# A three-layer decoder on one core: self slots in another order, a passage in another order, and idle TensorE on the identity at two places

## The reference

```
x = x + self_attention(layernorm(x))       # causal, 16 heads of 8, q = k = v = the normalised x
x = x + cross_attention(layernorm(x), ctx) # biased scores: q k^T + bias[b, h], projections Wq, Wk, Wv, Wo
x = x + ffn_block(layernorm(x))            # attention with projections, then a second norm,
                                           # a gate (argmax of 8 experts), expert w1, relu, w2
```

## Time and profile before

| what | us |
|---|---|
| median of 3 runs (lowest, highest) | 417.43 (417.13, 418.52) |
| the profiled execution, and its span | 417.45, 415.6 |
| start, to the first mask on VectorE (0 to 14.7): PE / DVE / ACT / POOL busy | 5.00 / 8.24 / 4.03 / 11.67 |
| self slots (14.7 to 74.8, 60.1 long) | 45.56 / 39.58 / 35.05 / 27.16 |
| passage (74.8 to 100.5, 25.7 long) | 17.84 / 17.35 / 10.34 / 11.57 |
| cross attention (100.5 to 200, 99.5 long) | 88.50 / 85.77 / 54.56 / 93.03 |
| last attention (200 to 310, 110 long) | 93.11 / 59.58 / 56.68 / 64.35 |
| gate and places (310 to 338, 28 long) | 12.74 / 10.24 / 5.94 / 4.23 |
| scatter of the rows (338 to 361.8, 23.8 long) | 0.01 / 1.03 / 0.00 / 15.66 |
| expert tiles (361.8 to 410, 48.2 long) | 47.19 / 34.02 / 24.80 / 21.06 |

### The profile page before, as it was taken

The page is one execution under the profiler, slowest core; times in us unless marked ns, Lnnn a source line. Parts: engine busy times, 40 slices in busy tenths (PEclk is TensorE's granted clock), DMA queues, the critical chain, the costliest instruction groups (busy, mean ns, idle before and its releaser), DMA issues.

```text
span 415.6 us, 9925 instructions
## 1 busy us (share of the span) xinstructions
PE 310.0 (75%) x3435; PEld 202.8 (49%) x3435; DVE 256.1 (62%) x614; ACT 191.4 (46%) x372; POOL 250.3 (60%) x354
## 2 busy tenths in 40 slices
PE   2677769568889999988788788888776400199993
PEld 0233335235666666656344444444444300199993
DVE  6667675667989999995357455656521340067772
ACT  2454566524655556554364365464661200045551
POOL 7943343276999889999958556673421237324453
PEclk9899999988999999999899899999995555589997
DMA  6103345003488787421139950000000012323430
GB/s 169 35 2 103 103 136 175 22 14 101 148 190 225 166 209 180 68 25 17 15 46 272 279 180 3 2 2 2 2 2 2 0 38 101 100 56 96 107 90 19
DMA packets 67041, 36.37 MB, mean 87 GB/s; under 512 B 36253, under 2 KB 56864, under 8 KB 66992
## 3 DMA queue, kind: packets, MB, share of 16 engines
q1 hardware_dynamic: 57040, 15.79, 17.8%
q10 hardware_dynamic: 8448, 16.78, 13.8%
q0 software_dynamic: 1504, 3.16, 2.2%
HBM read 28.48 MB, written 7.69 MB: 87 GB/s over the span
## 4 chain that ended last, share of the span: by engine, by line
PE 37%; POOL 26%; issue 16%; DVE 13%; ACT 5%; DMA 2%; POOLq 0%; DVEq 0%; ACTq 0%
PE pair_banks L605 24%; POOL biased L456 11%; PE work_bank L605 5%; POOL k_lane L433 4%; POOL routed_rows L588 4%; DVE pair_banks L1111 3%; PE small_bank L608 3%; POOL rstd L421 2%; DVE rowmax L1104 2%; PE small_bank L605 2%; PE work_bank L608 1%; ACT probs L944 1%; POOL shift L428 1%; POOL x_sb L482 1%; ACT outT L950 1%
## 5 line engine op out<-in xcount | busy, mean ns | idle before, releaser
L944 ACT ACTIVATE probs<-pair_banks 128x1024 f32<-128x1024 f32 x96 | 97.5, 1022 | 63.2 <-PE pair_banks L605 28.6
L456 POOL TENSOR_TENSOR biased<-biased,rowmax 128x1024 f32<-128x1024 f32 x32 | 60.3, 1896 | 10.6 <-DVE rowmax L1096 10.6
L605 PE MATMUL work_bank<-probs,vaug 128*32 128x128 f32 x1536 | 54.7, 286 | 5.2 <-ACT hn2T L958 3.4
L605 PEld LDWEIGHTS work_bank<-probs,vaug 128*32 128x32 f32 x1536 | 41.1, 114 | 23.0 <-issue 15.9
L415 POOL TENSOR_SCALAR vareps<-meanvar 128x2 f32<-128x2 f32 x32 | 8.2, 258 | 67.0 <-DVE meanvar L1054 65.7
L1104 DVE TENSOR_REDUCE rowmax<-pair_banks 128x8 f32<-128x1024 f32 x32 | 38.9, 1216 | 15.6 <-PE pair_banks L605 15.6
L1089 DVE TENSOR_TENSOR biased<-pair_banks,bias_in 128x1024 f32<-128x1024 f32 x32 | 38.8, 1213 | 12.1 <-PE pair_banks L605 11.7
L605 PE MATMUL pair_banks<-k_lane,qT 32*128 32x512 f32 x256 | 39.2, 683 | 4.8 <-issue 2.6
L595 POOL DMA_INDIRECT out<-vaug x23 | 22.6, 983 | 31.2 <-DVE vaug L1328 30.1
L1096 DVE TENSOR_REDUCE rowmax<-biased 128x8 f32<-128x1024 f32 x32 | 38.9, 1215 | 0.5
L605 PE MATMUL pair_banks<-q_lane,kT 32*128 32x512 f32 x256 | 38.1, 665 | 1.3 <-DVE biased L1089 1.3
(11 more groups left out here) (158 smaller groups left out, 574.1 us busy)
## 6 DMA issues: line engine op xcount, KB each, us to landing
bias_in<-in_w SPq DMA_DIRECT2D x16, 256.0 KB, 7.2
routed_rows<-filler SPq DMA_DIRECT2D x2, 1028.0 KB, 9.1
vaug<-routed_rows SPq DMA_DIRECT2D x23, 64.5 KB
biased<-routed_rows SPq DMA_DIRECT2D x23, 64.0 KB, 2.0
ctx_in<-in_ctx SPq DMA_DIRECT2D x8, 128.0 KB, 4.7
att_scratch<-att SPq DMA_DIRECT2D x16, 64.0 KB, 5.0
att_rows<-att_scratch SPq DMA_DIRECT2D x16, 64.0 KB, 2.8
routed_rows<-filler SPq DMA_DIRECT2D x1, 899.5 KB, 11.5
```

What stands on the lines that cost most here:

```text
L456: nc.gpsimd.tensor_tensor(v, v, rowmax[:, b % 2, 8 * half:8 * half + 8].unsqueeze(2).to_broadcast([128, 8, S]), ALU.subtract).then_inc(s_s ...
L605: return nc.tensor.matmul(o, lhsT, rhs, start=start, stop=stop, **kw)
L944: nc.scalar.activation(probs[:, b % 2, 2 * half:2 * half + 2, :], pair("exp", b, half), ACT.Exp, scale=1.0 if layer(b) == CROSS else SCALE ...
```

## The change

Six things are edited.

1. In a self slot TensorE does the row products directly behind the causal products, then the outputs of the slot before, then the output transposes, then a pair's transposes. ScalarE copies `outT` between the two exponentials. VectorE masks first and does the attention of two slots before afterwards.
2. In slots 14 and 15 TensorE makes the causal part of all four groups (`masked_by_pe`), so that VectorE masks nothing there; the preparation turns end with slot 13, and what was prepared in slots 14 and 15 uses the banks `work` and `small`.
3. Pairs 0 to 7 are all normalised on VectorE; statistics, normalising and the clearing of the values (now in quarters) of pairs 1 to 5 are spread over slots 0 to 4; the first queries are masked in two halves.
4. GpSimd's instructions for these pairs move with them.
5. `keep_awake(9)`: nine products of the identity with itself on TensorE ahead of the first transposes, into two banks that nobody uses at that time.
6. The scatter of batch 12 counts on its own semaphore (`s_nearly`); TensorE waits for it and does `keep_awake(24)` ahead of the first tile.

```diff
+def masked_by_pe(b):
+    return LAST_PREP < b < FIRST_CROSS
...
 def on_dve(q):
-    return 3 <= q < NP and player(q) == SELF
+    return q < NP and player(q) == SELF
...
-        if FIRST_PREP <= b < FIRST_CROSS:
+        if rotated(b):
             turns += [("prep", b, 0)]
...
             def causal_scores(b):
-                claim(PAIR_BANKS["exp", b, 0])
-                for g in range(2):
+                halves = 2 if masked_by_pe(b) else 1
+                for half in range(halves):
+                    claim(PAIR_BANKS["exp", b, half])
+                for g in range(2 * halves):
                     mm(bank_of("exp", b, g), identb[:], causal[:].rearrange("p g k -> p (g k)"), stop=False)
...
+            def keep_awake(times):
+                for n in range(times):
+                    mm(obk[n % 2][:, 0:S], ident[:], ident[:])
+
             pe.wait_ge(s_ident, 4)
-            for q in range(2):
-                claim("small")
-                self_transposes(q)
+            keep_awake(9)
+            self_transposes(0)
...
                     causal_scores(b)
-                    if b >= 2:
-                        out_transposed(b - 2)
-                    else:
-                        claim("small")
-                    if prepared(b) is not None and player(prepared(b)) == SELF:
-                        self_transposes(prepared(b))
                     self_scores(b)
                     if b >= 1:
                         add_outputs(b - 1)
+                    if b >= 2:
+                        out_transposed(b - 2)
+                    elif prepared(b) is not None:
+                        claim("small")
+                    if prepared(b) is not None:
+                        self_transposes(prepared(b))
...
             pe.wait_ge(s_route, 1)
+            pe.wait_ge(s_nearly, 16)
+            keep_awake(24)
             tile_transposed(0)
...
-            normalise(0)
-            normalise(1)
-            normalise(2)
...
+                if 0 <= b - 1 < FIRST_CROSS - 1:
+                    take_out(b - 1)
                 if b < FIRST_FFN:
                     exponentials(b, 1)
-                if 0 <= b - 1 < NB:
+                if FIRST_CROSS - 1 <= b - 1 < NB:
                     take_out(b - 1)
...
+                if b < FIRST_CROSS and not masked_by_pe(b):
+                    mask_second_half(b)
+                if b == 1:
+                    normalise(2)
+                    norm_stats(4)
                 if 0 <= b - 2 < NB:
                     attention(b - 2)
-                if b < FIRST_CROSS:
-                    if prepared(b) is not None and player(prepared(b)) == SELF:
-                        take_selfT(prepared(b))
-                    mask_second_half(b)
+                if b < FIRST_CROSS and prepared(b) is not None:
+                    take_selfT(prepared(b))
                 if 0 <= b - 2 < FIRST_CROSS:
                     self_residual(b - 2)
+                if b == 0:
+                    norm_stats(2)
+                    norm_stats(3)
+                if b < 3:
+                    clear_values(b + 1)
+                if b == 1:
+                    normalise(3)
```

More of the change, by code:

```diff
@@ L37 @@
 LAST_SLOT = 52
+LATE_BATCH = B - 4
 def layer(b):
@@ L549, in _ @@
                 if b == 0:
+                    inverse_deviation(2)
+                    self_queries(1)
                     inverse_deviation(3)
                     self_values(1)
-                    self_queries(2)
-                    self_values(2)
-                if b % 2 == 0 and q + 4 < NP and b < FIRST_CROSS:
-                    inverse_deviation(q + 4)
+                elif b < FIRST_CROSS:
+                    for m in measured_in(b):
+                        inverse_deviation(m)
                 if b in LAST_NORMS:
@@ L563, in _ @@
                         masked_queries(q + 2)
-                if b % 2 == 1 and q + 3 < NP:
-                    if player(q + 3) == SELF:
-                        self_queries(q + 3)
-                    (self_values, cross_residuals, ffn_residuals)[player(q + 3)](q + 3)
+                n = queried_in(b)
+                if b > 0 and n is not None:
+                    if player(n) == SELF:
+                        self_queries(n)
+                    (self_values, cross_residuals, ffn_residuals)[player(n)](n)
                 if b % 2 == 0 and q + 4 < NP and b >= FIRST_CROSS:
@@ L654, in v_products @@
                 b, bk = 2 * (q - 2), values_bank(q)
-                name = PAIR_BANKS["prep", b, 0] if b < FIRST_CROSS else "small" if cross else "work"
+                name = PAIR_BANKS["prep", b, 0] if rotated(b) else "small" if cross else "work"
                 claim(name)
@@ L938, in exponentials @@
             def exponentials(b, half):
-                if layer(b) == SELF and half == 1:
+                if layer(b) == SELF and half == 1 and not masked_by_pe(b):
                     act.wait_ge(s_masked, b + 1)
@@ L985, in _ @@
                     take_attT(c)
-                if normalised_in(b) is not None and b >= FIRST_FFN:
-                    normalise(normalised_in(b))
+                for n in normalised_in(b):
+                    if b >= FIRST_FFN:
+                        normalise(n)
                 if b in LAST_NORMS:
@@ L995, in _ @@
                     take_hT(q + 3)
-                n = normalised_in(b)
-                if n is not None and b < FIRST_FFN and not on_dve(n):
-                    normalise(n)
+                for n in normalised_in(b):
+                    if b < FIRST_FFN and not on_dve(n):
+                        normalise(n)
                 if FIRST_FFN <= b < NB:
@@ L1127, in attention @@
                 taken = prepared(b + 2) if b + 2 < FIRST_CROSS else None
-                if taken is not None and player(taken) == SELF:
+                if taken is not None:
                     dve.wait_ge(s_t, taken + 1)
@@ L1225, in _ @@
                     row_maxes(b + 2, 0, LAST_STEP)
-                if b % 2 == 0 and CROSS_PAIR <= q + 2 < NP and FIRST_CROSS <= b < FIRST_FFN:
+                if b % 2 == 0 and CROSS_PAIR <= q + 2 < NP and LAST_PREP < b < FIRST_FFN:
                     take_values(q + 2)
-                if b % 2 == 0 and q + 4 < NP:
-                    norm_stats(q + 4)
-                if normalised_in(b) is not None and on_dve(normalised_in(b)):
-                    normalise(normalised_in(b))
+                if b >= 2:
+                    for m in measured_in(b):
+                        norm_stats(m)
+                    for n in normalised_in(b):
+                        if on_dve(n):
+                            normalise(n)
                 if maxes:
@@ L1234, in _ @@
                     row_maxes(b + 2, 1, LAST_STEP)
-                if b % 2 == 0 and CROSS_PAIR <= q + 2 < NP and not FIRST_CROSS <= b < FIRST_FFN:
+                if b % 2 == 0 and CROSS_PAIR <= q + 2 < NP and not LAST_PREP < b < FIRST_FFN:
                     take_values(q + 2)
@@ L1239, in _ @@
             take_logits(7)
-            chain = [4]
+            chain = [6]
             def link(ins):
```

83 lines of the change are left out of this document (47 added, 36 removed).

## The result

The changed kernel takes 406.81 us (median of 4 runs, 403.75 to 407.17) against 417.28 for the kernel before beside it (416.99 to 418.52): a ratio of 0.9727, 95% interval 0.9676 to 0.9778. The prediction was 406.6 with a range of 401.5 to 411.5. The profiled execution has a span of 405.0 against 415.6, that is 10.6 less.

A forecast was written before the change was run, and what follows sets the result against it. It took waits between engines, chiefly a loop in the self slots, to bound the kernel, with no engine full. Sum: 417.45 - 10.6 (up to the cross scores) - 0.5 (passage) + 0.3 (expert tiles) = 406.6, range 401.5 to 411.5.

The forecast's parts named there:

- Start: Up to the first mask of the self slots: at 10.2 instead of 14.72, 4.5 earlier (bounds 3.5 and 5.0).
- Slots 0 to 4: First self slots: 22.5 in all, as before, since VectorE takes over preparation from the start; no gain.
- Slots 5 to 9: Steady self slots: 6.95 per pair, VectorE's work plus a residual held by q_lane; 6.95 + 7.75 = 14.7 against 17.8.
- Slots 10 to 13: Row products wait for the previous slot's second exponential, 3.7 a slot; 16.7 from mask 9 to cross scores, before 19.7.
- Passage: First cross scores to the steady cross loop's first biased scores: 21.9 against 22.4, -0.5 (ends -1.4 and +1.0).
- the second round takes up to 2.3 more: Passage: if TensorE comes back at the low clock after idling about 2.8, its second round lengthens by up to 2.3.
- the 24 that it named as a sign of being wrong: Passage: a length above 24 was listed among the signs that the prediction is wrong.
- Expert tiles: Start of the expert tiles: identity products delay first transposes 2.4, then full clock; first expert output +0.3 (-1.2 to +3.7).
- Its sign that the identity products end after 361.8: Ahead of the expert tiles: the 24 identity products ending after 361.8 was listed among the signs of being right.
- Pairs of 6.1: Rival 1, self slots: GpSimd and VectorE miss each other, pairs of 6.1 instead of 6.95, total 402.5; chance 0.17.
- the queues kept no wait ahead of a mask: Rival 2, slots 5 to 13: in-order queues keep part of the wait, 4.0 a slot, total about 411; chance 0.14.
- rival 4: Self slots: TensorE stays at the low clock, its 45.56 us of work taking 90; total 447, slower; chance 0.04.

The follow-up runs named there:

- the copy's 24.47: The changed kernel run again without any edit, beside three of the experiments: 411.32 us (406.48 to 414.38), ratio 0.9811 to the kernel before.

## Why the prediction was right, and where it was not

- **Start.** Said: first mask at 10.2, 4.5 earlier. Measured 9.84, 4.88 earlier. That VectorE's clears and not the row products hold it was right; without identity products it is 10.17.
- **Slots 0 to 4.** Said 22.5, measured 32.36 - 9.84 = 22.52. That this holds only with the new orders (the old ones with the same start need 4.7 more for the first four slots) I had not seen; I put it down as "no gain here".
- **Slots 5 to 9.** Said 6.95 and 7.75, measured 6.49 and 7.51. The mechanism, a residual held by `q_lane`, was right in place and length (1.50), and moving the `q_lane` away took 0.7 off a pair. What bounds the pair is VectorE, as said; its even slot, put at 3.15, took 2.83 (36.02 to 38.85). By the Trainium skill (SBUF — State Buffer, section Who interferes with whom), a VectorE instruction with two inputs in SBUF and a GpSimd instruction that reads SBUF block each other for a whole instruction. The trace agrees: the residual takes 1.50 under `q_lane` and 0.29 where that was moved away.
- **Which part opens the loop.** The prediction gave the copy and the order of TensorE together. In slots 9 to 13 either is enough: of 3.4 us the copy alone gives 2.7 and TensorE's order alone 3.4. The copy adds 0.0 to TensorE's order, and it can't stand in for it in the first slots, where the kernel without that order loses most of its time.
- **Slots 10 to 13.** Said 16.7 from mask 9 to the cross scores, measured 63.14 - 46.36 = 16.78. The row products of slots 11 to 13 start 0.05 to 0.17 after the second exponential of the slot before, as said; from mask to mask it is 1.93, 4.55, 3.75 and 3.76.
- **Passage.** Said 21.9, measured 23.5. The failing step is "the second round takes up to 2.3 more. I take 21.9": of the 2.3 for the low clock I took 0.9, and it was 2.5. The steps without it summed to 21.0, and with the clock held the passage took 20.99. Both measurements of the passage, 23.50 and the copy's 24.47, lie above the 23.3 that the prediction's own terms allowed at most, and the copy's passes the 24 that it named as a sign of being wrong.
- **Expert tiles.** Said +0.3, measured +0.8 in the changed kernel's profile (29.35 against 28.59), and -0.1 to +1.0 over the other kernels with these products (28.5 to 29.57); hold-back 2.1 instead of 2.4. The prediction's own terms (364.2 + 2.9 - 366.63) add up to +0.5, not to the +0.3 that it took. Its sign that the identity products end after 361.8 is a time of the kernel before; less the gain that it forecast up to there (11.1) it is 350.7, and they ended at 352.99.
- **The sum.** In the traces the self slots and the start gave 11.7 (said 10.6), the passage took 1.1 (said to give 0.5), the cross attention 0.3, the clock in the last attention took another 1.1 and gave 2.2 at the gate, and the tiles took 0.8. The agreement of 406.6 with 406.81 is therefore partly luck: two errors of 1.1 and 1.6 in the steps cancel, and the clock's 2.2 at the gate against 1.1 was in no step.
- **Rivals.** Pairs of 6.1 did not come by themselves, and in slots 5 to 10 the queues kept no wait ahead of a mask. The low clock of rival 4 did not come in the self slots (0.97), but it did come in the passage. The 49.5 us that rival 4 gives the stretch takes off the 4.5 of the start, which lies ahead of it; the prediction's own sum is 54.0, and 53.30 was measured.

## What to carry to other kernels

When an engine's order is changed, ask which engine's queue the waiting instruction stands in: here TensorE's order gave all of the gain in the later self slots, ScalarE's copy by itself gave most of it in slots 9 to 13 and added nothing to TensorE's order, and the earlier start was worth nothing without the new orders. Two edits that open the same loop do not add. Where a reader waits at the head of a queue with ready work behind it (VectorE's attention at the passage), moving the ready work ahead gave more than any other edit made on top of the change, and in one of two traces it kept TensorE's clock up as well. A product that only keeps a clock up pays where the engine idles anyway (2.5 in the trace of the passage) and not where it delays the work it is meant to speed (0 ahead of the tiles).

## What the runs showed of the hardware that was not expected

- The same instruction sequence takes 53.2 (two traces) or 55.2 to 55.4 us (twelve) from the last `k_lane` to the gate, by where in it the granted clock falls from 2.4 to 1.2 GHz (output projections 0.46 or 0.77 for the same pair).
- After an idle time of 2.49 TensorE came back low in the passage (1.92 for products of 1.14), but after 2.48 in the copy of the same kernel it stayed high for these products (1.14) and fell 3.0 later. The length of that one idle time does not say where the clock falls. With the idle time filled it stayed high through the passage (1.00).
- A normalisation on VectorE under a `q_lane` took 1.83 instead of 0.60 (17.92 of the changed kernel, 1.99 in an experiment): not only additions of two tiles in SBUF are held.
